# Four of 32 embedding tables held on chip, their rows picked by matmuls with one-hot columns

## The chip, the cores and the metric

The kernel runs on one NeuronCore of a Trainium2 chip. The metric is the device time of one execution in microseconds. The program is written engine by engine: TensorE (PE) for matmuls, VectorE (DVE) and ScalarE (ACT) for everything elementwise, GpSimd (POOL) for issuing gathers, SyncE (SP) for issuing plain loads. Each engine runs its own list in order; semaphores are the only link between them.

## The reference

512 samples, 32 categorical features, 256 numbers per embedding row, float32 throughout.

```python
e = stack([tbl_f[ids[:, f]] for f in range(32)], axis=1)     # [512, 32, 256]
dots = einsum('bnd,bmd->bnm', e, e)                          # 32x32 dot products of each sample
z = dots[:, iu, ju]                                          # the 496 above the diagonal
h = relu(concat([z, dense_ctx], 1) @ W_top1 + b_top1)        # 512 + 16 -> 512
h = relu(h @ W_top2 + b_top2)                                # 512 -> 256
y = h @ W_top3                                               # 256 -> 1
```

Ten tables have 12500 rows; the others have 1000 or 1250. The last four (features 28 to 31) have 1000, 1000, 1000 and 1250. The host concatenates all tables into one; this and the layout of weights are host work and not timed.

## The kernel before

**Tiles.** A tile is 4 samples by 32 features, 128 embedding rows on 128 partitions. There are 128 tiles, taken in 64 pairs. A unit is 8 tiles (4 pairs), a batch is 32 tiles (128 samples, 16 pairs, 4 units).

**The pipeline of a pair.** POOL issues one indirect DMA per tile (L201), which fetches 128 rows of 1 KB into a ring of 8 tiles (`RING`, L25). Before the gathers of pair p it waits until the pair p-4 has been transposed, since that frees the ring's places. PE transposes each tile by its two 128-column halves (L320, 4 instructions per pair) into one of two PSUM banks `xt_ps`. DVE copies the even pairs and ACT the odd pairs to SBUF (L213), into a ring of 8 pairs. PE then multiplies each transposed tile with itself (L341). A float32 matmul shows as two PE instructions, so the four matmuls of a pair's gram are 8 in the profile.

**The unit's end.** When 4 pairs are multiplied, DVE and ACT take the four 32x32 diagonal blocks of each tile from `gram_ps` (L232), DVE merges the two triangles (L242), and both spread the result into `z` by sixteen 32x32 copies (L190), nine on DVE and seven on ACT.

**The layers.** Two steps after a batch's last pair (`TURN`, L40: steps 18, 34 and 50) PE starts the first layer: in each of four steps one chunk of 128 outputs (context L366, 2 instructions, and four matmuls L379, 8 instructions), then the second layer (L387, 16) and the third (L396, 4) in one step each. ACT (L293) and DVE (L248) apply bias and relu. The last batch runs after the last pair, at the end, with 14 transposes of the identity ahead of it (L434).

**Order.** Each engine's order is written out by a loop over the pairs p. PE's step p is the transposes of p, the gram of p-1, then a layer's part if one is due. In DVE's and ACT's loops the copy of a pair and a unit's work follow each other, so a copy can stand behind a whole unit's work. PE's transposes of p wait for the copy of p-2 (two PSUM banks), its gram of p-1 for the copy of p-1.

**Loads.** SP loads ids and identity, waits for the first pair's transposes, and then issues `upper_sb` (the mask of L242), `ctx_sb`, `w1c_sb`, `w1z_sb` (1 MB), biases, `w2_sb` (512 KB) and `w3_sb` (L171 to L178).

Of the kernel before, what the change touches and what calls it, by code (L numbers as in the profile page):

```python
# [7 lines left out]
I32 = mybir.dt.int32  # L8
# [3 lines left out]
P = 128  # L12
# [9 lines left out]
PAIRS = TILES // 2  # L22
UNIT = 8
UNITS = TILES // UNIT
RING = 8  # L25
# [10 lines left out]
BATCHES = [(0, 32), (32, 32), (64, 32), (96, 32)]  # L36
LAST = len(BATCHES) - 1


TURN = [(first + tiles) // 2 + 2 for first, tiles in BATCHES]  # L40
LAST_UNIT = UNITS - 1
LAST_PAIR = PAIRS - 1
# [14 lines left out]
def ended_unit(p):  # L57

    return 2 * p // UNIT if (2 * p + 2) % UNIT == 0 else None


def samples(batch):
    first, tiles = BATCHES[batch]
    return slice(first * J, (first + tiles) * J)


def count(batch):
    return BATCHES[batch][1] * J


def dlrm_tower(nc, table, ids, eye, takes_upper, ctx_t, w1z, w1c, b1, w2, b2, w3, y):
    with ExitStack() as stack:
# [16 lines left out]
        upper_sb = sbuf("upper_sb", [P, UNIT, S], I32)  # L89
        xt = sbuf("xt", [P, XT_RING, 2, KD, P])  # L90
# [14 lines left out]
        mlp_ps = [psum(f"mlp_ps{i}", [P, 4, N]) for i in range(2)]  # L105
# [9 lines left out]
        w2_loaded = sem("w2_loaded")  # L115
        numbered = sem("numbered")
# [22 lines left out]
        def h1_ps(batch, n):  # L139
            if batch == LAST and n < 2:  # L140
                return xt_ps[n][:, 0, 0, 0:count(batch)]
            if batch == LAST:
                return gram_ps[0][:, UNIT // 2 * (n - 2)].rearrange("p j f -> p (j f)")[:, 0:count(batch)]
            return mlp_ps[n % 2][:, n // 2, 0:count(batch)]


        def tile_ps(n):
            return xt_ps[0][:, 0] if n == TILES - 1 else xt_ps[n // 2 % 2][:, n % 2]
# [3 lines left out]
        def product_ps(n):  # L152
            if n >= 2 * LAST_PAIR:
                return mlp_ps[0][:, n % 2, :]
            return gram_ps[n // UNIT % 2][:, n % UNIT].rearrange("p j f -> p (j f)")

        def h2_ps(batch, n):
            return mlp_ps[n][:, 2, 0:count(batch)]

        def y_ps(batch):  # L160
            return mlp_ps[0][0:1, 3, 0:count(batch)]
# [4 lines left out]
        def _(sp):  # L166
# [4 lines left out]
            sp.dma_start(upper_sb[:], takes_upper).then_inc(upper_loaded, 16)  # L171
# [12 lines left out]
        def spread(engine, copy, cells, done, u):  # L184

            engine.wait_ge(slots_ready, u + 1 if u < LAST_UNIT else u + 2)
            to = z[:].rearrange("p m (g j) -> p m g j", j=J)
            for j, q in cells:
                held = slots[F * j:F * j + F, u % 2, :, 0:S].rearrange("p g (m q) -> p m g q", q=Q)
                last = copy(to[F * q:F * q + F, :, UNIT * u:UNIT * (u + 1), j], held[:, :, :, q])  # L190
# [3 lines left out]
        def _(pool):  # L194
            for n in range(TILES):
                if n in (0, FIRST):
                    pool.wait_ge(numbered, 1 if n == 0 else 2)
                if n >= RING and n % 2 == 0:

                    pool.wait_ge(transposed, (n - RING) // 2 + 1)  # L200
                nc.gpsimd.indirect_dma_start(  # L201
                    rows[:, n % RING, :], None, table,
                    bass.IndirectOffsetOnAxis(ap=row_number[:, n:n + 1], axis=0),
                ).then_inc(rows_landed[n % RING], 16)

            spread(pool, nc.gpsimd.tensor_copy, LAST_CELLS[2], z_pool, LAST_UNIT)

        def copy_pair(engine, copy, p):
            if p >= XT_RING:

                engine.wait_ge(gram_ready, p - XT_RING + 1)
            engine.wait_ge(transposed, p + 1)
            copy(xt[:, p % XT_RING], xt_ps[p % 2][:]).then_inc(xt_ready[p % 2], 1)  # L213

        def copy_last(engine, copy, i):

            engine.wait_ge(gram_ready, LAST_PAIR - XT_RING + 1)
            engine.wait_ge(transposed, LAST_PAIR + 1 + i)
            copy(xt[:, LAST_PAIR % XT_RING, i], tile_ps(2 * LAST_PAIR + i)).then_inc(last_xt_ready[i], 1)

        def take_blocks(engine, copy, quadrants, u, tiles, pairs, done):
# [6 lines left out]
            for j in quadrants:  # L228
                held = gram_ps[u % 2][F * j:F * j + F, tiles, j, :]
                if pairs == PAIRS:  # L230
                    held = mlp_ps[0][F * j:F * j + F, 0:2, :].rearrange("p g (j f) -> p g j f", j=J)[:, :, j, :]
# [253 lines left out]
```

## Time and profile before

| | us |
|---|---|
| median of 3 runs | 211.35 (211.13 to 211.7) |
| the profiled execution's own time | 212.17 |
| its span, first to last instruction | 210.4 |
| PE busy | 152.6 |
| POOL busy | 122.7 |
| DVE busy | 76.4 |
| ACT busy | 64.3 |

Busy times of PE overlap (a matmul starts before the one before it has ended), so a busy PE is not PE at its peak. POOL's busy time is the issuing of 128 gathers. The DMA engines were busy for 31% of their time between 40 and 180 us.

### The profile page before, as it was taken

How to read it: one execution, taken by the hardware profiler on the slowest of the kernel's cores; microseconds unless marked ns; L12 is line 12 of the kernel's file. 1: busy time of each engine (PE TensorE's matmuls, PEld its weight loads, DVE VectorE, ACT ScalarE, POOL GpSimd, SP SyncE). 2: the span in 40 equal slices, each digit the busy share in tenths (PEclk: the TensorE clock that was granted, in tenths of full speed). 3: DMA queues.
4: the chain of work that ended last, by engine and by line, in shares of the span. 5: the costliest groups of instructions: out<-in, count | busy, mean ns of one | idle time of the engine just before them, and what ended most of it. 6: DMA issues, size and time to landing. Idle time of an engine off the chain costs nothing.

```text
span 210.4 us, 2889 instructions
## 1 busy us (share of the span) xinstructions
PE 152.6 (73%) x1022; PEld 136.9 (65%) x1022; DVE 76.4 (36%) x240; ACT 64.3 (31%) x194; POOL 122.7 (58%) x135
## 2 busy tenths in 40 slices
PE   0558177376858999676497979596598988666995
PEld 0358067276758898565386868585486878555894
DVE  0110160437162153734153153634162263616321
ACT  2011141335050261524133251515143251515241
POOL 4777475657577466757575657757575675751010
PEclk9996958969696799998569999978569999979799
DMA  1494233223323223323232332323232332321000
GB/s 44 131 352 148 75 99 104 62 88 98 101 80 101 76 79 90 108 75 100 75 103 75 100 100 76 101 76 102 72 108 74 97 101 76 100 75 50 3 0 0
DMA packets 7759, 18.80 MB, mean 89 GB/s; under 512 B 2593, under 2 KB 3489, under 8 KB 7618
## 3 DMA queue, kind: packets, MB, share of 16 engines
q0 software_dynamic: 6144, 16.79, 27.5%
q1 hardware_dynamic: 1602, 1.84, 2.8%
q8 instruction: 8, 0.13, 0.3%
q14 instruction: 5, 0.04, 0.1%
HBM read 18.62 MB, written 0.00 MB: 89 GB/s over the span
## 4 chain that ended last, share of the span: by engine, by line
PE 56%; issue 13%; another core or an unknown queue 11%; DVE 9%; ACT 7%; DMA 2%; POOL 1%; DVEq 0%; ACTq 0%
PE gram_ps L341 29%; PE xt_ps L320 12%; PE mlp_ps L379 5%; PE mlp_ps L387 4%; ACT z L190 4%; DVE slots L232 3%; DVE xt L213 2%; ACT xt L213 2%; PE mlp_ps L366 2%; DVE z L190 2%; DMA rows<-in_table,row_number 1%; PE mlp_ps L396 1%; DVE slots L242 1%; PE xt_ps L379 1%
## 5 line engine op out<-in xcount | busy, mean ns | idle before, releaser
L201 POOL DMA_INDIRECT rows<-in_table,row_number x128 | 121.7, 951 | 68.0 <-issue 33.0
L341 PE MATMUL gram_ps<-xt 128*128 128x128 f32 x504 | 83.9, 320 | 43.3 <-ACT xt L213 17.5
L341 PEld LDWEIGHTS gram_ps<-xt 128*128 128x128 f32 x504 | 75.0, 228 | 50.8 <-ACT xt L213 20.0
L213 DVE COPY xt<-xt_ps 128x512 f32<-128x512 f32 x32 | 22.1, 692 | 97.6 <-PE xt_ps L320 45.2
L320 PE MATMUL xt_ps<-identity,rows 128*128 128x128 f32 x256 | 48.1, 317 | 10.5 <-DMA rows<-in_table,row_number 10.5
L320 PEld LDWEIGHTS xt_ps<-identity,rows 128*128 128x128 f32 x256 | 36.4, 165 | 13.2 <-issue 7.0
L213 ACT COPY xt<-xt_ps 128x512 f32<-128x512 f32 x31 | 18.1, 585 | 57.1 <-remote 20.1
L190 DVE COPY z<-slots 32x32 f32<-32x32 f32 x142 | 31.6, 222 | 2.4
L190 ACT COPY z<-slots 32x32 f32<-32x32 f32 x111 | 27.2, 245 | 11.3 <-DVE slots L242 6.9
L232 ACT COPY slots<-gram_ps 32x256 f32<-32x256 f32 (+1 forms) x32 | 11.5, 361 | 45.6 <-PE gram_ps L341 18.2
L232 DVE COPY slots<-gram_ps 32x256 f32<-32x256 f32 (+1 forms) x32 | 13.1, 410 | 8.0 <-remote 2.8
L379 PE MATMUL mlp_ps<-z,w1z_sb 128*128 128x128 f32 x96 | 14.8, 301 | 0.0
L379 PEld LDWEIGHTS mlp_ps<-z,w1z_sb 128*128 128x128 f32 x96 | 12.4, 202 | 1.6 <-issue 0.4
L293 ACT ACTIVATE h_sb<-mlp_ps,b_sb 128x128 f32<-128x128 f32 x12 | 4.4, 369 | 22.4 <-PE mlp_ps L379 9.1
L387 PE MATMUL mlp_ps<-h_sb,w_sb 128*128 128x128 f32 x64 | 8.6, 279 | 0.8 <-ACT h_sb L293 0.8
L387 PEld LDWEIGHTS mlp_ps<-h_sb,w_sb 128*128 128x128 f32 x64 | 7.7, 192 | 1.3 <-ACT h_sb L293 1.0
L248 DVE TENSOR_SCALAR h_sb<-mlp_ps,b_sb 128x128 f32<-128x128 f32 x8 | 2.6, 349 | 12.0 <-PE mlp_ps L387 12.0
L366 PE MATMUL mlp_ps<-ctx_sb,w1c_sb 16*128 16x128 f32 x24 | 6.4, 349 | 0.0
L190 POOL COPY z<-slots 32x32 f32<-32x32 f32 x3 | 0.7, 246 | 9.6 <-DVE slots L242 9.5
L242 DVE COPY_PREDICATED slots<-upper_sb,slots 128x128 f32<-128x128 int32 (+2 forms) x17 | 5.0, 295 | 1.8
L366 PEld LDWEIGHTS mlp_ps<-ctx_sb,w1c_sb 16*128 16x128 f32 x24 | 3.9, 203 | 1.7 <-issue 0.4
L396 PE MATMUL mlp_ps<-h_sb,w_sb 128*1 128x128 f32 x16 | 2.4, 271 | 1.0 <-DVE h_sb L248 1.0
(26 smaller groups left out, 23.0 us busy)
## 6 DMA issues: line engine op xcount, KB each, us to landing
rows<-in_table,row_number POOLq DMA_INDIRECT x128
w1z_sb<-in_w1z SPq DMA_DIRECT2D x1, 1024.0 KB
w_sb<-in_w SPq DMA_DIRECT2D x1, 512.0 KB
ids_sb<-in_ids SPq DMA_DIRECT2D x1, 64.5 KB, 1.8
identity<-in_eye SPq DMA_DIRECT2D x1, 64.0 KB, 2.1
upper_sb<-in_takes_upper SPq DMA_DIRECT2D x1, 64.0 KB
ctx_sb<-in_ctx_t SPq DMA_DIRECT2D x1, 32.0 KB
w1c_sb<-in_w1c SPq DMA_DIRECT2D x1, 32.0 KB
```

The lines of the kernel that those rows point to most:

```text
L190: last = copy(to[F * q:F * q + F, :, UNIT * u:UNIT * (u + 1), j], held[:, :, :, q])
L201: nc.gpsimd.indirect_dma_start(rows[:, n % RING, :], None, table, bass.IndirectOffsetOnAxis(ap=row_number[:, n:n + 1], axis=0),).then_inc( ...
L213: copy(xt[:, p % XT_RING], xt_ps[p % 2][:]).then_inc(xt_ready[p % 2], 1)
L232: last = copy(slots[F * j:F * j + F, u % 2, tiles, :], held)
L242: nc.vector.copy_predicated(slots[:, u % 2, tiles, 0:S], upper_sb[:, tiles, :], slots[:, u % 2, tiles, S:F]).then_inc(slots_ready, 1)
L293: nc.scalar.activation(h1_sb[:, n, 0:count(batch)], h1_ps(batch, n), ACT.Relu, bias=b1_sb[:, n:n + 1]).then_inc(h1_ready, 1)
L320: done = nc.tensor.transpose(tile_ps(n)[:, k, :], rows[:, n % RING, k * P:(k + 1) * P], identity[:])
L341: done = nc.tensor.matmul(product_ps(n), x, x, start=(k == 0), stop=(k == KD - 1))
L366: nc.tensor.matmul(h1_ps(batch, n), w1c_sb[:, n * P:(n + 1) * P], ctx_sb[:, samples(batch)], start=True, stop=False)
L379: done = nc.tensor.matmul(h1_ps(batch, n), w1z_sb[:, m, n * P:(n + 1) * P], z[:, m, samples(batch)], start=False, stop=(m == MM - 1))
L387: last = nc.tensor.matmul(h2_ps(batch, n), w2_sb[:, k, n * P:(n + 1) * P], h1_sb[:, k, 0:count(batch)], start=(k == 0), stop=(k == KH1 - 1))
L396: last = nc.tensor.matmul(y_ps(batch), w3_sb[:, k:k + 1], h2_sb[:, k, 0:count(batch)], start=(k == 0), stop=(k == KH2 - 1))
```

## The change

**Features 28 to 31 of the batches 1 and 2 come from SBUF.** The four small tables are loaded whole (`hot_table`, 4.35 MB), each with 125 partitions of 8 (the last 10) consecutive rows. The ids of these features are loaded to all 125 partitions by one broadcast (`ids_bc`, 2000 pieces of 516 bytes). For each field and batch (8 in all) DVE compares the ids of 128 samples with the row numbers of each partition (`mark`: one operation over 125 x 1024 or 125 x 1280 elements) into `one_hot`. PE multiplies each chunk's 125 rows (two halves of 128 columns) with its one-hot columns and adds the chunks up in PSUM (`hot`: 34 chunks by 2 halves by 2 batches, 136 matmuls of 128 columns, 272 PE instructions). That gives the rows already transposed; ACT copies them into place, two fields at a time (`copy_hot`, 4 copies of 512 elements per partition).

**The gathers.** In batches 1 and 2 a tile is now 32 samples by 4 of the first 28 features, so that 28 tiles do for 128 samples instead of 32. The gathers go from 128 to 120, the pairs from 64 to 60. The transposed rows go to `hot_xt`, with a copy that reorders (strides of 32 elements on the write side). The grams of these two batches, still 4 samples by 32 features each, need pairs of the whole half batch, and are scheduled by the list `GRAMS`: one or two per step. POOL makes two small `iota` tables first; DVE makes the gather's row numbers for the new order (2 transposes, 16 small copies) before its first copy.

**Where the one-hot matmuls stand.** `HOTS` fills PE's steps from step 6 on: after the transposes, grams and layer parts of a step, as many one-hot matmuls follow as bring the step to 22 PE instructions. Worked out from the code, the steps 6 to 34 have 22 (one has 24), step 35 has 20, the steps 36 to 59 have no one-hot matmuls; field 0 begins in step 6, field 1 in 9, field 2 in 12, field 3 in 15. The layers begin in the steps 18, 38 and 51. In the steps 44 to 50 two grams stand in each step and a unit ends in every second one.

**Loads and PSUM.** `ids_bc`, the four tables and (behind the first of them) `upper_sb` go ahead of `ctx_sb` and `w1z_sb` on SP's queue. `hot_ps` takes one of the two `mlp_ps` banks, so PE waits in the first layer for the relu of the chunk before (it was the one before that).

```diff
+HOT = (1, 2)
+HOT_ROWS = (1000, 1000, 1000, 1250)
+HOT_P = 125
+CHUNKS = [r // HOT_P for r in HOT_ROWS]
...
+PAIR = [p for b in range(BATCHES)
+        for p in ([(b, v, i) for v in range(2) for i in range(GATHERS)] if b in HOT
+                  else [(b, t) for t in range(BT // 2)])]
...
+GRAMS = []
+for step in range(PAIRS):
+    at = sum(map(len, GRAMS))
+    due = [q for q in range(at, GRAM_PAIRS) if pairs_before(q) <= step]
+    GRAMS.append(due[:2] if len(due) >= UNIT or (len(due) > 1 and PAIR[step][0] not in HOT) else due[:1])
...
+SHARE = 22
+HOT_FROM = 6
...
+    many = max(0, (SHARE - passes(step)) // 2) if step >= HOT_FROM else 0
+    HOTS.append(HOT_LIST[at:at + many])
...
             sp.wait_ge(transposed, 1)
-            sp.dma_start(upper_sb[:], takes_upper).then_inc(upper_loaded, 16)
+            sp.dma_start(ids_bc[:], ids.rearrange("(j f) t -> j f t", f=F)[None, :, HOT_FIELD:F, :]
+                         .broadcast_to(ids_bc.shape)).then_inc(ids_bc_loaded, 16)
+            first = table.shape[0] - sum(HOT_ROWS)
+            for f in range(HF):
+                at = first + sum(HOT_ROWS[:f])
+                sp.dma_start(hot_table[:, CHUNK_AT[f]:CHUNK_AT[f] + CHUNKS[f], :],
+                             table[at:at + HOT_ROWS[f], :].rearrange("(p c) d -> p c d", c=CHUNKS[f])
+                             ).then_inc(hot_loaded[f], 16)
+                if f == 0:
+                    sp.dma_start(upper_sb[:], takes_upper).then_inc(upper_loaded, 16)
...
+            def mark(field):
+                h, f = divmod(field, HF)
+                c = CHUNKS[f]
+                if field == 0:
+                    dve.wait_ge(ids_bc_loaded, 16)
+                    dve.wait_ge(table_rows, 1)
+                if field >= 2:
+                    dve.wait_ge(hot_done, field - 1)
+                to = one_hot[:, field % 2, 0:c]
+                number = ids_bc[:, :, f, BT * HOT[h]:BT * (HOT[h] + 1)]
+                nc.vector.tensor_tensor(to, number[:, None].broadcast_to(to.shape),
+                                        table_row[c][:, :, None, None].broadcast_to(to.shape),
+                                        ALU.is_equal).then_inc(one_hot_ready, 1)
...
+                for u in ENDED[p]:
+                    unit(u)
+                for field in HOT_BEGINS:
+                    if p == (HOT_ENDS[field - 2] + 1 if field >= 2 else HOT_FROM - 2):
+                        mark(field)
...
+            def copy_hot(pair):
+                act.wait_ge(hot_done, 2 * (pair + 1))
+                nc.scalar.copy(hot_place(pair), hot_ps[:].rearrange("p f j k s -> p f (j k) s")).then_inc(hot_copied, 1)
...
+            def hot(field, k, c):
+                h, f = divmod(field, HF)
+                if k == 0 and c == 0:
+                    if h == 0:
+                        pe.wait_ge(hot_loaded[f], 16)
+                    pe.wait_ge(one_hot_ready, field + 1)
+                    if field >= 2 and field % 2 == 0:
+                        pe.wait_ge(hot_copied, field // 2)
+                done = nc.tensor.matmul(hot_ps[:, field % 2, :, k, :], hot_table[:, CHUNK_AT[f] + c, k * P:(k + 1) * P],
+                                        one_hot[:, field % 2, c], start=(c == 0), stop=(c == CHUNKS[f] - 1))
+                if k == KD - 1 and c == CHUNKS[f] - 1:
+                    done.then_inc(hot_done, 1)
...
             for p in range(LAST_PAIR):
                 transposes(p)
-                if p:
-                    gram(p - 1)
+                for q in GRAMS[p]:
+                    gram(q)
...
-                        if n >= 2:
-                            pe.wait_ge(h1_ready, batch * KH1 + (n - 1))
+                        if n:
+                            pe.wait_ge(h1_ready, batch * KH1 + n)
...
+                for field, k, c in HOTS[p]:
+                    hot(field, k, c)
```

## Rows read from the trace of the kernel before

**Rows 1.** The page: the gathers' group; busy us, mean ns, idle before by releaser.

```profile
L201 POOL DMA_INDIRECT rows<-in_table,row_number x128 | 121.7, 951 | 68.0 <-issue 33.0
```

**Rows 2.** Timeline: POOL's first and last gather, and one wait for the ring.

```profile
3.04 1.11 POOL L201 DMA_INDIRECT rows<-in_table,row_number  x1 [2.60 <-DVE row_number L263]
...
99.69 0.94 POOL L201 DMA_INDIRECT rows<-in_table,row_number  x1 [0.30 <-issue]
...
102.61 0.94 POOL L201 DMA_INDIRECT rows<-in_table,row_number  x1 [1.97 <-remote]
...
189.24 0.95 POOL L201 DMA_INDIRECT rows<-in_table,row_number  x1 [0.30 <-issue]
```

**Rows 3.** Timeline around one unit's end (us 94 to 103), PE, DVE, ACT.

```profile
94.03 0.84 DVE L232 COPY slots<-gram_ps 32x256 f32<-32x256 f32 x2
...
95.32 2.17 DVE L190 COPY z<-slots 32x32 f32<-32x32 f32 x9
...
97.12 0.59 ACT L213 COPY xt<-xt_ps 128x512 f32<-128x512 f32 x1
...
97.76 1.54 PE L341 MATMUL gram_ps<-xt 128*128 128x128 f32 x8 [2.00 <-issue]
...
102.44 0.69 DVE L213 COPY xt<-xt_ps 128x512 f32<-128x512 f32 x1 [4.95 <-remote]
```

**Rows 4.** Timeline of PE in steps of 22 instructions (first layer of a batch).

```profile
115.92 0.48 PE L366 MATMUL mlp_ps<-ctx_sb,w1c_sb 16*128 16x128 f32 x2
...
117.33 0.60 PE L320 MATMUL xt_ps<-identity,rows 128*128 128x128 f32 x4
117.76 1.06 PE L341 MATMUL gram_ps<-xt 128*128 128x128 f32 x8
118.75 0.48 PE L366 MATMUL mlp_ps<-ctx_sb,w1c_sb 16*128 16x128 f32 x2
```

**Rows 5.** Granted clock (PEclk) of two stretches; busy us of each engine.

```profile
71.10:98.30 27.20, 21.72 (x177) 19.92 (x177) 14.03 (x44) 11.24 (x35) 18.00 (x19) 1.00 0.33 93
98.50:108.50 10.00, 6.97 (x33) 6.57 (x33) 2.01 (x4) 1.22 (x3) 6.51 (x7) 0.50 0.30 91
```

**Rows 6.** Timeline: w1z's load issued; PE waits for a gather issued at 9.47 us.

```profile
9.26 0.42 SPq L174 DMA_DIRECT2D w1z_sb<-in_w1z  x1
9.47 0.95 POOL L201 DMA_INDIRECT rows<-in_table,row_number  x1 [0.30 <-issue]
...
14.77 0.44 PE L320 MATMUL xt_ps<-identity,rows 128*128 128x128 f32 x2 [2.17 <-DMA rows<-in_table,row_number]
```

**Rows 7.** DMA queues, 11 to 13.5 us: packets, MB, share of 16 engines.

```profile
DMA packets 102, 0.84 MB, mean 348 GB/s; under 512 B 0, under 2 KB 0, under 8 KB 0
q1 hardware_dynamic: 102, 0.84, 85.9%
```

**Rows 8.** The same, 14 to 15 us (w2's pieces of 1 KB).

```profile
q1 hardware_dynamic: 343, 0.35, 98.6%
```

**Rows 9.** The page: packets of SP's queue, whole span.

```profile
q1 hardware_dynamic: 1602, 1.84, 2.8%
```

**Rows 10.** Timeline: the transposes of pair 16 and of pair 62.

```profile
56.38 1.06 PE L320 MATMUL xt_ps<-identity,rows 128*128 128x128 f32 x4
...
190.78 0.60 PE L320 MATMUL xt_ps<-identity,rows 128*128 128x128 f32 x4
```

**Rows 11.** DVE's groups by form: busy us, mean ns, idle before.

```profile
L190 DVE COPY z<-slots 32x32 f32<-32x32 f32 x142 | 31.6, 222 | 2.4
L213 DVE COPY xt<-xt_ps 128x512 f32<-128x512 f32 x32 | 22.1, 692 | 97.6 <-PE xt_ps L320 45.2 <-PE gram_ps L341 25.2 <-remote 20.5
L219 DVE COPY xt<-xt_ps 128x256 f32<-128x256 f32 x1 | 0.4, 425 | 3.7 <-PE xt_ps L320 3.7
```

**Rows 12.** Timeline: DVE's first copy, and the first use of the mask.

```profile
7.96 0.69 DVE L213 COPY xt<-xt_ps 128x512 f32<-128x512 f32 x1 [5.01 <-PE xt_ps L320]
...
26.89 0.30 DVE L242 COPY_PREDICATED slots<-upper_sb,slots 128x128 f32<-128x128 int32 x1
```

More of the change, by code:

```diff
@@ L54 @@
 TAKES_UPPER = np.where(LANE < S, LANE >= SLOT, LANE - S < SLOT)
-def ended_unit(p):
-    return 2 * p // UNIT if (2 * p + 2) % UNIT == 0 else None
 def samples(batch):
[L63 to L68, printed above, removed]
+    return slice(batch * N, (batch + 1) * N)
 def dlrm_tower(nc, table, ids, eye, takes_upper, ctx_t, w1z, w1c, b1, w2, b2, w3, y):
@@ L115, in dlrm_tower @@
         w2_loaded = sem("w2_loaded")
+        ids_bc_loaded = sem("ids_bc_loaded")
+        hot_loaded = [sem(f"hot_table{f}_loaded") for f in range(HF)]
+        table_rows = sem("table_rows")
+        one_hot_ready = sem("one_hot_ready")
+        hot_done = sem("hot_fields_done")
+        hot_copied = sem("hot_field_pairs_copied")
+        turned = sem("row_numbers_turned")
+        hot_numbered = sem("hot_numbered")
         numbered = sem("numbered")
@@ L194, in _, with gather @@
         def _(pool):
[L195 to L200, printed above, removed]
+            for c, rows_of in table_row.items():
+                done = nc.gpsimd.iota(rows_of[:], [[1, c]], base=0, channel_multiplier=c)
+            done.then_inc(table_rows, 1)
+            def gather(n, numbers):
                 nc.gpsimd.indirect_dma_start(
-                    rows[:, n % RING, :], None, table,
-                    bass.IndirectOffsetOnAxis(ap=row_number[:, n:n + 1], axis=0),
+                    rows[:, n % RING, :], None, table, bass.IndirectOffsetOnAxis(ap=numbers, axis=0),
@@ L298, in unit @@
                 spread(act, nc.scalar.copy, ACT_CELLS, z_act, u)
+            def copy_hot(pair):
+                act.wait_ge(hot_done, 2 * (pair + 1))
+                nc.scalar.copy(hot_place(pair), hot_ps[:].rearrange("p f j k s -> p f (j k) s")).then_inc(hot_copied, 1)
             for p in range(LAST_PAIR):
-                if p and ended_unit(p - 1) is not None:
-                    unit(ended_unit(p - 1))
+                for pair in range(HF * len(HOT) // 2):
+                    if p == HOT_ENDS[2 * pair + 1] + 1:
+                        copy_hot(pair)
+                for u in ENDED[p]:
+                    unit(u)
                 if p % 2 == 1:
```

196 lines of the change are left out of this document (143 added, 53 removed).

## The prediction

> **What bounds the kernel now.** I read the page's groups first, then POOL's timeline, then the timeline around the end of a unit, then the DMA queues.
>
> A gather takes POOL 0.95 us and the next is issued 0.30 us later [rows 1, 2], so 1.25 us each, 160 us for 128. The first starts at 3.04 us and the last at 189.24 us [rows 2]: 186.2 us, or 1.466 each. The reader should see that POOL's floor explains 159 of 186 us and waits for the ring of 8 tiles the other 27. POOL's idle total of 68.0 us [rows 1] is misleading, since half of it is the 0.30 us between issues. One such wait is 1.97 us before the gather at 102.61 [rows 2]; spread over 16 units it is 1.7 us each.
>
> The waits come from the end of a unit. DVE spreads a unit until 97.49, ACT too, and the copies of transposed pairs stand behind: ACT's copy starts at 97.12 and PE, idle for 2.00 us, goes on at 97.76. Then DVE's next copy starts only at 102.44, after 4.95 us of idling for a release that the profile can't name, and POOL's gather follows 0.17 us later [rows 2, 3]. So a lag between PE's transposes and their visible release belongs to this stall, and I can't explain it. PE then also runs at the lower clock: 0.50 (1.2 GHz) from 98.50 to 108.50 after the pauses, 1.00 (2.4 GHz) from 71.10 to 98.30, where it was mostly busy [rows 5].
>
> The whole is a pace: pair 16 is transposed at 56.38 us, pair 62 at 190.78 [rows 10], 2.92 us per pair where POOL alone would need 2.51. After 190.78 come 19.6 us to the end of the span.
>
> **The change, part by part.** The sum is made against the profiled execution: span 210.4, own time 212.17, so 1.8 outside the span; the median 211.35 is 0.8 below it. I add 1.0 to a span to compare with the median.
>
> *Gathers.* Eight fewer. At POOL's floor that is 8 x 1.25 = 10.0 us, at today's pace 11.7.
>
> *PE.* 272 instructions are added, four pairs' transposes (16) go. At full clock one costs 0.11 us: four transposes fill 117.33 to 117.76, a gram's eight 117.76 to about 118.65 [rows 4]. 256 x 0.11 = 28 us more PE work, placed behind each step's other work. A step of 22 with ten one-hot instructions takes 22 x 0.11 = 2.44 us at best. The nearest existing step of 22, with a layer's chunk, takes 118.75 - 115.92 = 2.83 us [rows 4], of which 0.4 is around the context matmul of 16 rows, which a one-hot step lacks. Since POOL needs 2.51 per pair, bounds are 2.51 and 2.92 (no gain); I take 2.65. It should mean that the filler covers the unit's end: a copy is late by DVE's or ACT's unit of some 3 us, and PE now has 1.1 us of filler in each of two steps plus the other work. Where the cover fails, the step stays at 2.92.
>
> *DVE.* `mark` has no row. From 425 ns for 256 elements and 692 for 512 [rows 11] the slope is 1.04 ns per element, so 1.22 us for 1024 and 1.49 for 1280, eight marks 10.3 us (two inputs from SBUF could make it up to double; a faster mode half). A unit's work is 3.5 us (94.03 to 97.49 [rows 3]), with two copies of 0.69 per four steps; with one mark 6.2 of 10 us. Hidden. If not, one mark late shifts one copy by 1.3 us. The row-number work (18 operations; small ones take 0.22 [rows 11], 4 us) fits the 5.01 us of idling before DVE's first copy [rows 12]. The two iotas fit POOL's 2.60 us before the first gather [rows 2]; a stall there would be paid in full, and I bound it at 0 to 2 us.
>
> *Copies.* 28 copies write with strides. No row has a large strided write; the 32x32 copies take 0.22 us for 32 elements per partition [rows 11], which is mostly fixed cost. Bounds are 0.69 and double that; hidden in DVE's 97.6 us of idling before copies [rows 11]. ACT's four `copy_hot` likewise. The earlier relu wait in the layers (three per batch, relu 0.4 us) is hidden by the next step's transposes and gram, 1.3 us, unless ACT is in a unit: up to 2 us per batch, three times at most. I count 0.
>
> *Loads, the largest term.* 4.35 MB of tables and 1.03 MB of ids go ahead of `w1z`. From 11 to 13.5 us 0.84 MB went in pieces of 8 KB with 85.9% of 16 engines busy [rows 7]: 34.4 engine-us, 24.4 KB per engine-us. The tables need 178 engine-us. A 1 KB piece took 0.986 x 16 / 343 = 46 ns [rows 8]; 2000 pieces of 516 bytes need between 46 (by bytes) and 92 engine-us (by piece), I take 60.
>
> Over how many engines? SP's queue had 1602 packets [rows 9]. The loads have 1441 pieces (seven of 128, two of 16, `w2`'s 512, `out_y`'s one). The other 161 fit a closing packet from each engine used: ten loads with 16, and `out_y`, one piece, with 1. So a load is cut into equal shares over partitions. The largest divisor of 125 up to 16 is 5. I take 5 engines: 178 / 5 = 35.6 us and 60 / 5 = 12.0. The bounds are 16 engines (11.1 and 3.8) and 5.
>
> The load starts about 9.3 us, the time of `w1z`'s issue today [rows 6]. Gathers share the engines: 8 KB on each engine, 0.33 us, some 32 of them until then, 10.5 us. The last table lands at 9.3 + 12.0 + 35.6 + 10.5 = 67.4 us. Step 15 begins field 3 and waits for it; today pair 16 is at 56.38. The tables before it, one per 9.5 us or so, pace the steps 6 to 15, and the mask, used at 26.89 today [rows 12], comes only after the first table at about 33 us; both lie inside that wait. `w1z` then has 3 us to arrive before step 18 needs it, 8 us later.
>
> The Trainium skill, DMA: Bandwidth & Descriptors, section "Why a DMA increments its semaphore by 16 and not by 1", says that such a load uses the largest number of engines up to 16 that divides the slowest dimension. By it the count is 5, as taken above; no load of before has such a shape.
>
> *The sum.* Step 16 begins at 67.8. Twenty steps (16 to 35) at 2.65: 53.0. Twenty-two (36 to 57) at today's 2.92: 64.3. From step 58, the counterpart of pair 62, to the end: 19.6. Span 204.7, plus 1.0: 205.7, say 206 us. The eight gathers and the faster steps win 17 us, the loads give 11 back.
>
> **Rivals.**
>
> *Loads wide or early enough (A).* With 16 engines the last table is there before 30 us and nothing waits. The steps 6 to 15 gain 2.7 too: 53.7 + 53.0 + 64.3 + 19.6 + 1.0 = 191.6; with a slower pace up to 197. For it: every large load of before used 16. Against it: 125.
>
> *Starved gathers (C), slower than before.* From 11 to 13.5 us the 102 packets were all SP's [rows 7], not one of a gather's, though POOL was issuing; the gather of 9.47 us reached PE at 14.77 [rows 6] after 5.3 us, of which it idled 2.17 for it. `w1z` puts 8 pieces on an engine and went as one block of 2.4 us. A table puts 25 there, 7.1 us. If a block lets one or two gathers pass, then about 10 gathers land during 35.6 us of tables instead of 26. Before the tables about 13 have landed, at 60 us 23. Pair 16 needs 34: eleven more at POOL's 1.25 us, 74.5 us. 74.5 + 53.0 + 64.3 + 19.6 + 1.0 = 212.4; with 18 landed instead 219. It decides against the change when fewer than about 24 have landed by 60 us. Against it: a queue of small turns would share evenly, and a late table hides some of a late gather.
>
> The Trainium skill's same page, section "Queues, rings and completion order", says that an engine goes round its queues by packets of some 9 to 17 descriptors and at most 64. By that a gather waits for more than one 8 KB piece at a time but not for a whole load of 25, which lies between my forecast and this rival.
>
> *The unit's stall stays (D).* If the unexplained lag persists with filler, the 20 steps cost 2.92: 211, no change. For it: no row says what the lag comes from, so none says that filler removes it; against it, the copies behind a unit are a sufficient cause for PE's own pauses. The seven two-gram steps (a unit every second step: DVE 4.2 of 5 us) could add 2 to 3 us in each case.
>
> **How the numbers follow.** Forecast 0.42, A 0.20, C 0.28, D 0.10. The forecast's own range is 200 to 212 (ids 9 to 18 us, pace 2.51 to 2.92). A measurement tells 0.3%, 0.6 us, from no change. Faster: A 0.20, forecast 0.34, C 0.03, D 0.03. No change: 0.06. Slower: C 0.24, forecast 0.05, D 0.05. The range 194 to 217 leaves out A's low end and C's high end.
>
> **What would show it.** Packets of SP's queue: about 5 closing ones for each of five new loads. PE idle in the steps 6 to 15 for `hot_table` loads, until about 67 us. POOL's last gather near 183 us. Gathers' waits in the first 65 us: PE waiting for rows instead of tables is rival C. Steps 20 to 35 at about 2.65 us without POOL's waits and with the clock at 1.00; 2.92 with waits is D. The prediction is wrong if the tables are there by 35 us, or if the one-hot matmuls cost clearly more than 0.11 us each.

## The result, and the profile after

The changed kernel takes 220.49 us (median, 218.56 to 222.9), the kernel before 211.52 on the same chip: a ratio of 1.037, interval 1.025 to 1.049. It is slower by 9.0 us, where 206 (194 to 217) was forecast. The profiled execution took 218.56 us, its span is 216.8.

The page of the changed kernel; queue rows are packets, MB and share of 16 engines, the others are groups as in [rows 1] and [rows 11]:

```profile
q1 hardware_dynamic: 2627, 7.23, 10.4%
...
L301 POOL DMA_INDIRECT rows<-in_table,row_number x64 | 61.9, 967 | 40.0 <-PE xt_ps L483 17.5
L301 POOL DMA_INDIRECT rows<-in_table,hot_number x56 | 55.7, 995 | 36.7 <-PE xt_ps L483 21.0
...
L521 PE MATMUL hot_ps<-one_hot,hot_table 125*128 125x128 f32 x272 | 38.6, 289 | 10.8 <-ACT hot_xt L458 10.0
...
L330 DVE COPY hot_xt<-xt_ps 128x512 f32<-128x512 f32 x14 | 14.6, 1045 | 44.7 <-PE xt_ps L483 31.1
...
L336 DVE COPY xt<-xt_ps 128x512 f32<-128x512 f32 x16 | 11.1, 691 | 37.4 <-PE xt_ps L483 22.7
...
L415 DVE TENSOR_TENSOR one_hot<-ids_bc,table_row 125x1024 f32<-125x1024 int32 (+1 forms) x8 | 10.2, 1285 | 1.0 <-PE hot_ps L521 0.9
```

POOL's idle before its gathers rose from 68.0 us [rows 1] to 76.7, though eight gathers are gone. The work that was added costs what was forecast or a little more (the prices stand below), so the loss has to be looked for in the waits too. SP's queue first (SPq: start, length, load):

```profile
8.11 0.33 SPq L258 DMA_DIRECT2D ids_bc<-in_ids  x1
8.48 0.85 SPq L263 DMA_DIRECT2D hot_table<-in_table  x1
9.37 3.89 SPq L267 DMA_DIRECT2D upper_sb<-in_takes_upper  x1
13.30 12.53 SPq L263 DMA_DIRECT2D hot_table<-in_table  x3
25.88 0.33 SPq L268 DMA_DIRECT2D ctx_sb<-in_ctx_t  x1
26.24 9.16 SPq L269 DMA_DIRECT2D w1c_sb<-in_w1c  x1
35.45 0.57 SPq L270 DMA_DIRECT2D w1z_sb<-in_w1z  x1
```

`w1z` is issued at 35.45 instead of 9.26 [rows 6], the issues before it being held up. From 62 to 71 us SP's queue is still busy for 26.7% of 16 engines, 85% of five. What that does first is seen at the mask, in the timeline (start, length, engine, line; in brackets the idle time before and what ended it):

```profile
33.37 0.30 DVE L367 COPY_PREDICATED slots<-upper_sb,slots 128x128 f32<-128x128 int32 x1 [4.61 <-DMA upper_sb<-in_takes_upper]
...
36.14 2.08 PE L509 MATMUL gram_ps<-xt 128*128 128x128 f32 x8 [8.63 <-ACT xt L336]
```

The mask was used at 26.89 [rows 12] and is used at 33.37; DVE and ACT stand at it, and PE stands 8.63 us behind them. The rest of PE's way to pair 16 has one more long stop, and only at its end a short one for a table:

```profile
59.39 1.62 PE L521 MATMUL hot_ps<-one_hot,hot_table 125*128 125x128 f32 x6 [5.35 <-ACT hot_xt L458]
...
69.85 0.71 PE L521 MATMUL hot_ps<-one_hot,hot_table 125*128 125x128 f32 x4 [0.78 <-issue]
```

The last table's packets end at 69.1 us, so pair 16 could not come earlier than it does (70.4), but in this execution the mask and the wait for `copy_hot` (L458, the copy of picked rows out of PSUM) took up nearly all of the time that PE would have waited for tables. Further on in the timeline, undisturbed steps with one-hot matmuls and a stop:

```profile
98.95 0.60 PE L483 MATMUL xt_ps<-identity,rows 128*128 128x128 f32 x4
99.39 1.06 PE L509 MATMUL gram_ps<-hot_xt 128*128 128x128 f32 x8
100.28 1.28 PE L521 MATMUL hot_ps<-one_hot,hot_table 125*128 125x128 f32 x10
101.40 0.60 PE L483 MATMUL xt_ps<-identity,rows 128*128 128x128 f32 x4
101.83 1.06 PE L509 MATMUL gram_ps<-hot_xt 128*128 128x128 f32 x8
102.73 1.06 PE L521 MATMUL hot_ps<-one_hot,hot_table 125*128 125x128 f32 x8
...
103.56 1.01 ACT L330 COPY hot_xt<-xt_ps 128x512 f32<-128x512 f32 x1
...
107.28 1.01 ACT L458 COPY hot_xt<-hot_ps 128x512 f32<-128x512 f32 x1 [2.71 <-remote]
...
108.44 0.77 PE L521 MATMUL hot_ps<-one_hot,hot_table 125*128 125x128 f32 x2 [4.66 <-ACT hot_xt L458]
```

A step takes 2.45 us (98.95 to 101.40), as forecast for its best. Then PE waits for `copy_hot`, and ACT, free from 104.57, starts it only at 107.28: PE's one-hot matmuls had ended at 103.79 by the record, and their release came about 3.5 us later. The next place like it, at DVE and POOL together:

```profile
135.68 1.01 DVE L330 COPY hot_xt<-xt_ps 128x512 f32<-128x512 f32 x1 [6.97 <-remote]
...
135.91 0.95 POOL L301 DMA_INDIRECT rows<-in_table,hot_number  x1 [1.68 <-remote]
```

DVE's copy and POOL's gather wait for the transposes of pair 36, which by the record had ended at 131.6. This is the lag of 102.44 and 102.61 in [rows 2, 3]; it has stayed. I call it a late release below: more than 0.3 us between the recorded end of a pair's transposes and the release that its copy then follows. Among the 38 pairs of the kernel before for which the trace lets the two be matched, 23 are late, 59.5 us in sum; in the changed kernel 15 of about 40, 33.4 us. Windows of the changed kernel (columns as in [rows 5]), steps 16 to 35 and 36 to 57:

```profile
70.30:130.90 60.60, 53.99 (x443) 52.16 (x442) 27.89 (x65) 22.52 (x51) 37.58 (x38) 0.94 0.30 88
131.00:198.60 67.60, 59.39 (x451) 55.05 (x450) 32.39 (x104) 30.29 (x85) 40.53 (x43) 0.92 0.30 86
```

In the first window PE is busy for 54.0 of 60.6 us. Its waits there, in full, from the view of waits (us in total, times, longest):

```profile
PE hot_ps L521 <- ACT hot_xt L458: 4.7, 1, 4.7
PE mlp_ps L556 <- ACT h_sb L448: 1.3, 1, 1.3
PE mlp_ps L556 <- DVE z L291: 0.7, 1, 0.7
```

The same twenty steps of the kernel before (56.4 to 117.3 us) have PE busy for 47.4 of 60.9 us, and all its waits stand before a gram, which waits for the copy of its pair (for 9.1 us of them the profile names no releaser):

```profile
PE gram_ps L341 <- issue: 9.1, 5, 2.0
PE gram_ps L341 <- DVE xt L213: 3.0, 1, 3.0
PE gram_ps L341 <- ACT xt L213: 1.3, 1, 1.3
```

Set against the sum of the prediction:

| stretch | forecast | measured | before |
|---|---|---|---|
| to pair 16's transposes | 67.8 | 70.4 | 56.4 |
| steps 16 to 35 | 20 x 2.65 = 53.0 | 60.6 (3.03 each) | 60.9 (3.05 each) |
| steps 36 to 57 | 22 x 2.92 = 64.3 | 67.6 (3.07 each) | 62.4 (2.84 each) |
| four more pairs (58 to 61), before only | | | 11.0 |
| step 58 (before: 62) to the end | 19.6 | 18.2 | 19.6 |
| span | 204.7 | 216.8 | 210.4 |

The forecast took 2.92, the mean of all pairs from 16 to 62, for the steps of before; its steps 16 to 35 take 3.05 and its steps 36 to 57 2.84. The start cost 14.0 us more than before, of which 11.4 were forecast. The four pairs less gave back 11.0, the steps 16 to 35 gave nothing, and the steps 36 to 57 cost 5.2 more. Against the forecast, 10.9 of the 12.1 us by which the sum is short lie in the pace.

### The profile page after: what moved, and what is told of

Read it like the earlier page. It is cut to its first block, busy times and chain, and to the rows that moved or that the text cites. A ratio compares the mean times of both kernels' runs of the same rounds, so it can differ in the third digit from the quotient of the medians.

```text
span 216.8 us, 3430 instructions
## 1 busy us (share of the span) xinstructions
PE 168.8 (78%) x1278; PEld 157.6 (73%) x1278; DVE 90.0 (42%) x264; ACT 73.8 (34%) x196; POOL 118.7 (55%) x129
## 3 DMA queue, kind: packets, MB, share of 16 engines
q1 hardware_dynamic: 2627, 7.23, 10.4%
## 4 chain that ended last, share of the span: by engine, by line
PE 59%; another core or an unknown queue 10%; issue 9%; ACT 7%; DVE 6%; POOL 5%; DMA 4%; DVEq 0%; ACTq 0%
PE gram_ps L509 25%; PE hot_ps L521 11%; PE xt_ps L483 10%; POOL rows L301 5%; PE mlp_ps L568 4%; PE mlp_ps L576 3%; DMA rows<-in_table,row_number 3%; ACT z L291 3%; PE mlp_ps L556 2%; DVE slots L357 1%; ACT hot_xt L458 1%; ACT xt L336 1%; PE mlp_ps L586 1%; DVE hot_xt L330 1%
## 5 line engine op out<-in xcount | busy, mean ns | idle before, releaser
L301 POOL DMA_INDIRECT rows<-in_table,row_number x64 | 61.9, 967 | 40.0 <-PE xt_ps L483 17.5
L301 POOL DMA_INDIRECT rows<-in_table,hot_number x56 | 55.7, 995 | 36.7 <-PE xt_ps L483 21.0
L483 PE MATMUL xt_ps<-identity,rows 128*128 128x128 f32 x240 | 42.3, 300 | 12.7 <-DMA rows<-in_table,row_number 12.7
L509 PE MATMUL gram_ps<-xt 128*128 128x128 f32 x248 | 38.8, 307 | 14.7 <-ACT xt L336 12.3
L509 PEld LDWEIGHTS gram_ps<-xt 128*128 128x128 f32 x248 | 35.2, 219 | 16.8 <-ACT xt L336 13.1
L521 PE MATMUL hot_ps<-one_hot,hot_table 125*128 125x128 f32 x272 | 38.6, 289 | 10.8 <-ACT hot_xt L458 10.0
L521 PEld LDWEIGHTS hot_ps<-one_hot,hot_table 125*128 125x128 f32 x272 | 35.6, 205 | 11.3 <-issue 10.3
L509 PE MATMUL gram_ps<-hot_xt 128*128 128x128 f32 x256 | 35.6, 291 | 3.8 <-DVE hot_xt L330 3.8
L509 PEld LDWEIGHTS gram_ps<-hot_xt 128*128 128x128 f32 x256 | 33.5, 207 | 4.0 <-DVE hot_xt L330 4.0
L330 DVE COPY hot_xt<-xt_ps 128x512 f32<-128x512 f32 x14 | 14.6, 1045 | 44.7 <-PE xt_ps L483 31.1
L336 DVE COPY xt<-xt_ps 128x512 f32<-128x512 f32 x16 | 11.1, 691 | 37.4 <-PE xt_ps L483 22.7
L330 ACT COPY hot_xt<-xt_ps 128x512 f32<-128x512 f32 x14 | 14.7, 1048 | 21.4 <-PE xt_ps L483 17.2
(41 smaller groups left out, 67.8 us busy)
```

Of the source, the lines that this page charges most:

```text
L301: nc.gpsimd.indirect_dma_start(rows[:, n % RING, :], None, table, bass.IndirectOffsetOnAxis(ap=numbers, axis=0),).then_inc(rows_landed[n % ...
L330: copy(to, held).then_inc(xt_ready[p % 2], 1)
L336: copy(xt[:, place % XT_RING], xt_ps[p % 2][:]).then_inc(xt_ready[p % 2], 1)
L483: done = nc.tensor.transpose(tile_ps(n)[:, k, :], rows[:, n % RING, k * P:(k + 1) * P], identity[:])
L509: done = nc.tensor.matmul(product_ps(t), x, x, start=(k == 0), stop=(k == KD - 1))
L521: done = nc.tensor.matmul(hot_ps[:, field % 2, :, k, :], hot_table[:, CHUNK_AT[f] + c, k * P:(k + 1) * P], one_hot[:, field % 2, c], start ...
```

## The experiments

The runs fell on five chips, and these differ by kind, so each result is read against the kernel before on its own chip. On three (the result's, B and E) the kernel before takes 211.5, 212.1 and 217.4 us, on two (A and D) 180.4 and 180.3 (the letter C stands for a theory, not for a chip). The theories: **L**, the tables come over five engines and pace the start. **R**, the release lag stays and eats the pace. Against them **C**, the loads starve the gathers, and **M**, the one-hot matmuls and their copies are themselves too dear.

### Chip A (before: 180.38 us)

**e1: both kinds of loads split into 112 and 13 partitions.**

```diff
+for part in (slice(0, 112), slice(112, HOT_P)):
+    sp.dma_start(hot_table[part, CHUNK_AT[f]:CHUNK_AT[f] + CHUNKS[f], :], ...
```

> The changed kernel with each of its five new loads issued as two, for the partitions 0 to 111 and 112 to 124; nothing else differs. Theory (the loads run on as many engines as divides the partitions: 5 for 125, 16 for 112 and 13 for 13): SP's queue shows 29 closing packets per load instead of 5, the last table lands before 35 us instead of at about 69, pair 16 is transposed at 55 to 58 us instead of 70.3, and the time falls by 12 to 15 us, to about 206. Rival (gathers are starved whatever the number of engines, since the bytes are the same): pair 16 not before 64, time 214 or more. Second rival (the wait for the tables only hid other stalls): pair 16 comes early but the end does not, gain under 5 us.

195.03 us, ratio 1.080 (1.073 to 1.087). The waits of PE, from the view of waits (us in total, times, longest):

```profile
PE xt_ps L486 <- DMA rows<-in_table,row_number: 20.8, 13, 6.3
```

Pair 16 is transposed at 64.2 us, and the last table is there at 46.0 us, not before 35. The packets are as the theory has them (2747, which is 120 more, 24 for each load). So wide loads don't make the start short: the wait for tables turns into a wait for gathers, as the first of the two rivals had it. Rival C's mechanism is real once the loads are wide.

**e2: only the mask's load ahead of ids and tables.**

```diff
 sp.wait_ge(transposed, 1)
+sp.dma_start(upper_sb[:], takes_upper).then_inc(upper_loaded, 16)
...
-    if f == 0:
-        sp.dma_start(upper_sb[:], takes_upper).then_inc(upper_loaded, 16)
```

> The changed kernel with the mask (upper_sb) loaded ahead of the ids and tables, nothing else. Theory: the mask's wait (DVE 4.6 us, until 33.4) is gone and the steps 6 to 9 come up to 4 us earlier, but step 15 still waits for the last table at 68 to 69 us; pair 16 stays at 69 to 71, time within 1.5 us of the changed kernel. Rival (the stall of the first unit is what the start costs): time 4 to 5 us lower.

202.59 us (one execution), a ratio of 1.12. Pair 7 comes at 36.9 us, 2.9 earlier than in the profile above, pair 16 at 71.5, no earlier: the tables hide the mask. PE waits for tables for 13.0 us in all here. What this run shows beside that is the pace of the same code on the other kind of chip. The window of steps 16 to 35, and from its timeline the wait that took 4.66 us above:

```profile
71.40:125.80 54.40, 52.62 (x442) 50.91 (x441) 28.11 (x65) 23.52 (x52) 37.80 (x38) 0.97 0.33 98
```

```profile
103.43 1.06 PE L520 MATMUL hot_ps<-one_hot,hot_table 125*128 125x128 f32 x8
106.27 0.46 PE L520 MATMUL hot_ps<-one_hot,hot_table 125*128 125x128 f32 x2 [1.78 <-ACT hot_xt L457]
```

2.72 us a step, close to the forecast's 2.65, and 2.52 in the steps 36 to 57; one or two transposes of some 40 are late, where the same instructions gave 15 on the other chip.

**e3: wide loads, mask first, and only the first and last chunk of each field multiplied (104 of 136 matmuls out).**

```diff
+if c not in (0, CHUNKS[f] - 1):
+    return
```

> Wide loads and the mask first, and PE leaves out the one-hot matmuls of all chunks but a field's first and last: 32 matmuls instead of 136 (208 PE instructions fewer). If PE's added work sets the pace of the steps 16 to 35 (3.03 us each in the changed kernel), they fall to 2.6 or less and the time is 6 to 10 us under the wide kernel. If late releases, the longer reordering copies or copy_hot set it, the steps stay at 2.9 and the time within 3 us of the wide kernel.

188.91 us (one execution). Steps 16 to 35 take 2.39 us instead of e1's 2.68, and the time is 6.1 us under e1's: both lie where the first branch had them, so on this chip PE's added work does set the pace of these steps. It does so for 0.03 us per instruction left out, where one takes 0.11 at full clock, so most of the filler stands in time that PE would idle anyway. Scaled to all 136 matmuls, an estimate from these two runs, M is worth some 8 us on a chip of this kind; on the other kind no run tells.

**e4: the kernel before with a ring of 16 tiles.**

```diff
-RING = 8
+RING = 16
```

> The kernel before with a ring of 16 gathered tiles instead of 8. If POOL's waits for the ring are the bound (27 of 186 us), the last gather starts at 165 to 170 us and the time falls by 10 to 20 us. If PE, held by the copies at each unit's end and by releases that come late, is the bound, POOL runs ahead but PE keeps 2.9 us per pair: the last gather starts earlier, the time stays within 3 us of 211.5.

180.49 us, ratio 0.999 (0.997 to 1.002). The page's group of its gathers:

```profile
L201 POOL DMA_INDIRECT rows<-in_table,row_number x128 | 121.2, 947 | 41.4 <-issue 37.2
```

POOL's idle is 41.4 us instead of 68.0 [rows 1], the 0.30 us between issues and little else; the gathers run from 3.2 to 162.1 us, POOL's floor. Pair 16 to pair 62 takes 115.0 us, 2.50 a pair, and none of 43 matched transposes is late. On such a chip the kernel before is at POOL's pace, and the run can't decide between the two cases.

### Chip B (before: 212.07 us)

**r5: the changed kernel itself.**

> The changed kernel itself, beside the kernel before on whatever chip this is. The kernel before took 211.5 us on the first chip and 180.4 us on the second, where POOL never waited. Theory: the changed kernel loses most where the kernel before is at POOL's floor: about 202 us against 180 (12% slower) on such a chip, 220 against 211 on one like the first. Rival: the ratio of 1.037 holds on every chip, 187 us against 180.

221.39 us, ratio 1.049 (1.042 to 1.056), 17 of 40 late (35.8 us). The result repeats. PE's idle time in the steps 16 to 35 is 5.7 us, all of it at waits for `copy_hot`. On a chip where before takes 180.4 us the changed kernel itself never ran; e2 comes closest there and fits the theory's 202.

**r6: the kernel before with the five new loads added, into buffers that nothing reads.**

```diff
+sp.dma_start(ids_bc[:], ...).then_inc(extra_loaded[4], 16)
+for f, c in enumerate((8, 8, 8, 10)):
+    sp.dma_start(hot_table[:, 8 * f:8 * f + c, :], ...).then_inc(extra_loaded[f], 16)
```

> The kernel before with only the five new loads added, in the changed kernel's order and shape (125 partitions), into buffers nobody reads; the program waits for them at its end. If the gathers are starved by these loads, pair 16 is transposed at 60 us or later (46.2 without them on the second chip) and the time rises by 14 us or more. If in the changed kernel only the waits for the tables and the mask matter, gathers pass almost freely: pair 16 by 52 us (the mask still comes at about 33 us), time up by 3 to 6 us.

223.19 us (one execution), 11.1 over the kernel before, whose executions lie between 210.5 and 214.0. The mask on DVE and `w1z` on PE:

```profile
33.59 0.29 DVE L255 COPY_PREDICATED slots<-upper_sb,slots 128x128 f32<-128x128 int32 x1 [6.39 <-DMA upper_sb<-in_takes_upper]
...
76.21 0.79 PE L379 MATMUL mlp_ps<-ctx_sb,w1c_sb 16*128 16x128 f32 x2 [4.35 <-DMA w1z_sb<-in_w1z]
```

Pair 16 is at 62.2 us, six later than [rows 10]; PE stands 8.54 us behind the mask between the pairs 6 and 7. From pair 7 (38.2) to pair 16 a pair takes 2.67 us, and PE's waits for rows come to 19.0 us where the kernel before has 10.5 and the changed kernel 12.7. So the gathers are slowed a little while the loads run over five engines, and C is not what holds the kernel as it is. Neither branch came true whole: pair 16 fits the first, the time lies between the two. The queue again has 2627 packets. The loads alone cost 11.1 us: six by pair 16, the rest in the next twenty pairs, where `w1z` is waited for. All the rest of the change (eight gathers fewer, filler, marks, copies) gives back 223.19 - 221.39 = 1.8, which is no more than the executions of one kernel differ. The forecast had 11 and 17: the loads' term was about right in size, the gain's was not.

**r7: wide loads, mask first, tables in pieces of 1 KB (row c x 125 + p on partition p).**

```diff
-.rearrange("(p c) d -> p c d", c=CHUNKS[f])
+.rearrange("(c p) d -> p c d", c=CHUNKS[f])
```

> The wide kernel with the mask first and the tables laid out so that a piece is one row of 1 KB instead of 8 KB (row c*125 + p on partition p, the row numbers of the iota to match). If gathers starve because an engine serves a block of large pieces before it turns to them, the tiles 4 and 5 come 3 us or more earlier (pair 2 at 19.1 us in the wide kernel) and pair 16 before 58 us (64.1). If it is the bytes in front of them, pair 16 stays at 62 to 66.

208.46 us (one execution), with 16.6 us of PE's waits for rows. Pair 16 comes at 62.5 us, where the second branch had it (the bytes in front of the gathers), and pair 2 at 16.5, 2.7 earlier than in e1, just short of the first branch's 3.

**r8: the same, each table held back until 1, 4, 7 and 10 pairs are transposed.**

> The same with SP waiting before the tables for 1, 4, 7 and 10 transposed pairs, so that a table of 1 MB goes out about every 8 us. Theory (a burst of loads starves the gathers, spread out they share): pair 16 at 50 to 54 us, time 11 to 14 us under the wide kernel's 195, that is 182 to 185 where the kernel before takes 180.4. Rival: PE waits for the late tables instead, pair 16 at 58 or later, time 188 or more.

214.76 us, ratio 1.018 (1.011 to 1.026). Pair 16 stands at 62.5 us in r7 and r8 alike, as the rival had it: holding tables back gains nothing there.

### Chip D (before: 180.32 us)

> The kernel before with a ring of 16 tiles instead of 8. Chips have shown two levels of the kernel before: 211 to 212 us, with 23 of 38 matched transposes released 0.3 us or more after their recorded end (59.5 us in sum), and 180.4 us, with none late. This run tells something on a chip of the first kind. Theory R (a late release costs because the gathers stand behind the ring): 16 tiles bridge a lag of up to 6.6 us, POOL comes back to 1.25 us a gather, and the time falls to 185-198. Theory P (the late releases hold PE itself, through the copies of the transposed pairs, whatever the ring): 207-213, ratio to before 0.98 to 1.01. On a chip of the second kind both say 180-181 again.

> The changed kernel with the mask first, loads split into 112 and 13 partitions and pieces of 1 KB, as in the single look that took 208.46 us beside 212.07 before. Timed here in three rounds. If that gain was real on a chip where the kernel before takes 211 to 212: 206-211, ratio 0.97 to 0.995. If it was an execution's luck: 211-217. On a chip where before takes 180.4: 190-196, since there before is at POOL's own pace and the loads and the one-hot matmuls can only add.

> The kernel of the run before this one, with a ring of 16 tiles. Theory R: 16 tiles bridge the late releases, 3 to 8 us under the kernel with 8 tiles (199-205 on a chip of 211-212). Theory P: the late releases hold PE through the copies, within 2 us of the kernel with 8 tiles (206-211).

r12 leaves out fourteen of sixteen cells of each unit's spread:

```diff
-spread(dve, nc.vector.tensor_copy, DVE_CELLS, z_dve, u)
+spread(dve, nc.vector.tensor_copy, DVE_CELLS[:1], z_dve, u)
...
-spread(act, nc.scalar.copy, ACT_CELLS, z_act, u)
+spread(act, nc.scalar.copy, ACT_CELLS[:1], z_act, u)
```

> The kernel before with z set to zero once at the start, and each unit but the last spreading two of its sixteen 32x32 cells (one on DVE, one on ACT) instead of sixteen: the other cells of z stay zero, so the output leaves most of the dot products out. Theory U (the engines' work at a unit's end, DVE and ACT busy 3 to 4 us each, is what makes PE's releases late): on a chip of 211-212 the late releases go (under 5 of some 40) and the time falls to 182-195. Theory H (the late releases are not made by that work): at least 12 remain late, 30 us or more in sum, and the time is 200-211. On a chip of 180.4: 179-181 in both.

r9 180.43 (1.002, 0.999 to 1.005), r10 191.4 (1.065, 1.059 to 1.070), r11 189.29 (1.051, 1.046 to 1.057), r12 180.1. At most one transpose is late in each. The chip was of the quick kind, so r9 and r12 decide nothing; r10 shows that even the better loads leave the change 11 us slower where before is at POOL's floor.

### Chip E (before: 217.44 us)

> As r9, in the hope of a chip where the kernel before takes 211 to 212 us. Theory R (a late release costs because the gathers stand behind the ring of 8 tiles): 185-198, ratio 0.88 to 0.94. Theory P (the late releases hold PE itself, through the copies of the transposed pairs): 207-213, ratio 0.98 to 1.01. On a chip of 180.4: the third reading of 1.00, which says nothing.

224.08 us, ratio 1.031 (1.022 to 1.039): slower, which neither theory had. 18 of 37 transposes are late (47.8 us), so the ring doesn't bridge them. That falls against theory R; of theory P only this much holds, that the ring doesn't matter to the late releases. Part of the extra comes from one stop at the start (DVE):

```profile
34.81 0.69 DVE L213 COPY xt<-xt_ps 128x512 f32<-128x512 f32 x1 [18.38 <-issue]
```

Pair 4 had been transposed by 20.9 us, and the profile can't name what its copy waits for until 34.81. In the profiled execution of the kernel before that copy started at 25.34.

> As r12: each unit but the last spreads two of its sixteen cells, the other cells of z stay zero, so most dot products are left out. On a chip of 211-212: theory U (the engines' work at a unit's end makes PE's releases late): under 5 late of some 40, 182-195. Theory H (it does not): at least 12 late, 30 us or more in sum, 200-211. On a chip of 180.4: 180 in both.

210.68 us (one execution beside a median of 217.44), and 33 of 47 late, 93.6 us in sum. PE, DVE and POOL:

```profile
95.17 0.60 PE L321 MATMUL xt_ps<-identity,rows 128*128 128x128 f32 x4
...
102.44 0.69 DVE L213 COPY xt<-xt_ps 128x512 f32<-128x512 f32 x1 [5.74 <-PE gram_ps L342]
...
102.61 0.94 POOL L201 DMA_INDIRECT rows<-in_table,row_number  x1 [1.41 <-PE xt_ps L321]
```

DVE's work at the unit's end is one cell of 0.18 us here instead of nine, and pair 30 is still released 6.57 us late; it was 6.58 in the execution of [rows 3] and 6.68 in r13. Theory U falls and theory H's numbers came true: the engines' work at a unit's end doesn't make the lag. Leaving most of it out does shorten the time, by 6.8 us.

> As r10. On a chip of 211-212: 206-211, ratio 0.97 to 0.995 if the gain of the single look (208.46 beside 212.07) was real, 211-217 if not. On a chip of 180.4: 190-192 again, ratio 1.06.

216.45 us median, 211.56 to 221.92, before 216.0 to 221.22. The executions scatter too widely for a ratio; the gain of 3.6 us that r7's one execution had is neither confirmed nor refuted, and no version of mine is shown to beat the kernel before.

> The changed kernel itself. On a chip of 211-212: 219-223, ratio 1.04 to 1.05, a third reading. On a chip of 180.4, where it has not run yet: the same kernel with the mask first took 202.6 there, and the mask's wait until 33 us (8.6 us of PE) comes on top only so far as the tables do not hide it, so 202-206, ratio 1.12 to 1.14. If the change's cost were an absolute 9 us on every chip: 189-191.

222.05 us, ratio 1.022 (1.013 to 1.031). The third chip on which the change costs 4.6 to 9.3 us; 27 of 45 late (60.2 us). In the steps 16 to 35 PE idles for 4.0 us, 3.8 of them at `copy_hot`.

## Why the prediction was wrong

**The loads: right in size, partly by luck.** Five closing packets for each of five new loads: 1602 [rows 9] + 375 table pieces of 8 KB + 125 of 10 KB + 500 of 2 KB for `ids_bc` + 25 = 2627. For `ids_bc` I had counted 2000 pieces of 516 bytes. The bytes are the same, and so was the time. The last table lands at 69.1 us for 67.4 forecast, and e2 puts pair 16 at 71.5 on another chip. By the rule of the Trainium skill that the prediction cited (DMA: Bandwidth & Descriptors, "Why a DMA increments its semaphore by 16 and not by 1") five engines were due, and the packet count agrees. That the mask would lie inside the tables' wait was right too (e2). The sign that I had named, PE idle for tables until about 67 us, did not show as such: PE waits 0.8 us for one in the result's execution, 6.9 in r5, 5.6 in r16 and 13.0 in e2, since the mask and `copy_hot` stop it first. And that r6 prices the loads at 11.1 us and the forecast at 11.4 is luck: in r6 nothing waits for a table, and the price is made up of the mask, `w1z` and slower gathers.

**The pace: the step that failed.** "I take 2.65. It should mean that the filler covers the unit's end." The steps 16 to 35 took 3.03 us, no less than the same steps of before (3.05). Of the 7.6 us by which this term was short, 1.0 is PE's own work: 54.0 us busy, 2.70 a step at a mean clock of 0.94, so a step of 22 instructions fills more than 2.65 us even without a pause. The other 6.6 us are the idle time shown above, and 6.0 of them are waits that the change brings with it and that I had put at nothing: `copy_hot` ("likewise" hidden, 4.7 us) and the relu of the chunk before (1.3 us). The stop that the filler was meant to cover is covered: PE doesn't wait once for the copy of a pair in these steps, where before it idled 13.5 us at them. r5 and r16 have the same picture, with 5.7 of 5.7 and 3.8 of 4.0 us of idle time at `copy_hot`.

The release lag stands behind that wait: ACT starts `copy_hot` 3.5 us after the recorded end of what it waits for, and PE's wait took 4.66 us, against 1.78 at the same place in e2, where nothing near it is late and ACT starts the copy 0.6 us after that end, busy until then. Filler can't cover this one, since it is the filler's own result that is released late and the next filler that waits. The same twenty steps take 2.72 us in e2, 1.4 us in all above the forecast; the other 6.2 is the difference between the two kinds of chip, in which the late releases are what the traces show. No run takes them away on one chip, so their share of it is argued and not shown.

In the steps 36 to 57, which have no filler, PE's longest wait (3.83 us) is for the copy of pair 36, released 4.0 us late; e2 has 2.52 us a step there, the result's execution 3.07. Rival D, which I gave 0.10, was right that the lag stays and nearly right in the price of a step, and wrong about the place: it had PE held at the copies behind a unit.

**D's size was low too.** It had the steps at 2.92 and 211 us. The changed kernel was above that by 0.11 and 0.15 a step, 5.6 us over 42 steps, and by 2.6 at the start. Against the steps of the same numbers before, only 36 to 57 are dearer, by 0.23 each. What makes them so, beside pair 36, is not settled: the 28 reordering copies take 1.05 us instead of 0.69 and 0.59, in bounds, and PE has 1278 instructions instead of 1022.

**Rival C.** The price (212.4) was nearest to the result, and the mechanism was not it, so that is luck: PE's waits for rows came to 12.7 us in the whole execution, against 10.5 before, and r6 has 2.67 us a pair under the loads. It comes up with wide loads (20.8 us in e1, 16.6 in r7). How many pieces pass at one turn, the rule of the Trainium skill that was set beside it (DMA: Bandwidth & Descriptors, "Queues, rings and completion order"), no run here shows.

**Rival A.** Wide loads came near its 192 to 197 (195.03, 191.4, 189.29), but only on chips where the kernel before takes 180. There the quantity to beat was POOL's floor, and A's reasoning (start as before, then faster steps) fails: the start stays at 59.8 to 64.2 us against 46.2.

**Single costs.** One-hot matmuls 2.45 us for an undisturbed step of 22 (forecast 2.44). `mark` 1.22 and 1.49 us (1.22 and 1.49). The copies 1.05 us (0.69 to 1.38). The iotas cost nothing at the first gather, which starts at 3.2 us as before.

**What the prediction could have done.** It named the lag in [rows 3] and could not explain it, and then let the likeliest case rest on its going away, without asking which new waits of PE would stand behind such a release. An idle of 4.95 us whose releaser the profile can't name is a cost that may come back at another wait; priced at its own size it gives 67.8 + 42 x 2.92 + 19.6 + 1.0 = 211, no change, before any other error. And a pace of 2.65 us left 0.2 us a step over the 2.45 of undisturbed work, with no term for the lower clock.

## What to carry to other kernels

Filler can cover a stop and bring the next one with it: here it took PE's 13.5 us of waits for pairs out of twenty steps and put 22 instructions a step and a wait for `copy_hot` in their place, for no gain. So add up the work of a filled step first, and then go through the waits that the filler itself needs, above all those in which it waits for its own earlier result by way of another engine. Price bulk loads by ablation, adding them unread to the kernel before: that run gave a loss of 11.1 us, and left a gain of 1.8 for all the rest, too small for one execution to show. And compare only within a chip: 180.4 and 212.1 us for one kernel is more than any version here was worth.

## What was not expected of the hardware

**Late releases.** On three of five chips releases of PE's semaphores come up to 7.3 us after the recorded end of the matmul (pair 47 of r14), on two none or one or two per execution. They don't depend on a place in time but on a place in the program: pairs 26, 30, 31 and 34 are late in the kernel before, in r6, in r13 and in r14, on three chips, pair 30 by 6.58, 6.52, 6.68 and 6.57 us. Of the 23 in the kernel before, 17 begin at a granted clock of 1.00, so a low clock isn't needed for one; for pair 30 the drop to 0.50 ([rows 5], 98.50) comes after its recorded end (95.76) and before its release (102.35). The Trainium skill (Perfetto Trace Analysis, "Summary: the profiler window per engine type") says that the end of a TensorE instruction is an estimate and that the propagation of its semaphore is hidden from the profile. The trace says a little more. In the kernel before, the transposes of pair 30, the gram of pair 29 and the transposes of pair 31 have recorded ends of 95.76, 99.30 and 100.15 us, and are released at 102.35, 102.44 and 102.50: in the program's order, within 0.15 us, in which PE can't have done eight matmuls and four transposes (1.54 and 1.06 us by the record). In r6 and r13 the three come within 0.15 us of each other too. So at least the earlier of them are held back after the work is done, and not only recorded too early. What holds them back stays open, and so does whether the profiler has a part in it: on these chips the trace also lacks some of the semaphore's updates (60 in the kernel before, where e4 and r9 have 66).

**A deeper ring can cost.** 16 tiles instead of 8 changed nothing on two chips (0.999, 1.002) and cost 3.1% on a third. Its profiled execution has the one long stop of DVE at the start that is shown above; whether the others have it, and what it comes from, is open.
